# The last stage of a vision and state-space kernel: decays in two pairs of banks, one scan over two groups, the sum added to h by TensorE and ScalarE

## The chip, the cores and the metric

One core of one Trainium2 chip. The metric is the time of one execution on the device in microseconds. All data are float32.

## What is computed

The reference has three parts. A tokenizer (two performer layers between unfoldings of the image) gives tokens h of width 768, 3136 tokens for each of 4 images. Then a selective state-space layer is added to h, and then a routed mixture of 8 experts. Cut to what the change touches:

```
x     = layernorm(h)
Bproj = x @ W_B + b_B;  Cproj = x @ W_C + b_C          # 16 states each
delta = softplus(x @ W_D + b_D + p_Delta)              # one per channel
A_bar = exp(delta * A)
B_bar = (A_bar - A) / (delta * A) * delta * Bproj
state = A_bar * state + B_bar * x                      # over the tokens, in order
y     = sum over the 16 states of Cproj * state
h     = h + y
h     = h + experts(layernorm(h))
```

## The kernel before

Three stages run one after the other. The change is in the third, `tail`. It goes over 28 rounds (`UNITS`, i): 4 images times 7 pieces of 448 tokens (`T`). A round has 24 slots (`STEPS`, k): 6 chunks of 128 channels (dc) times 4 quarters of the states (q). In a slot the 128 partitions hold 32 channels times 4 states, and four groups g of 448 tokens hold the other channels of the chunk. So one slot is 128 x 4 x 448 numbers in one tile of the ring `v` (`RING` = 5 tiles). State by state the work of a slot is:

1. GpSimd, `weigh_in` (L1450): v = x * B, one product of 128 x 1792. It waits until TensorE has read the tile five slots back.
2. ScalarE, `step` (L1691): decay = exp(delta * A) into PSUM, one group at a time, into three banks in turn. The fourth group needs the scan of the first.
3. VectorE, `weigh` (L1793): v = (decay - A) * v, and `scan` (L1802), the recurrence over 448 tokens. Group by group, a scan is issued one `weigh` behind its own, so the last scan of a slot stands behind the first `weigh` of the next and behind all other work of the slot.
4. ScalarE, `keep_states` (L1681): the last column of v goes to `st`, where the scan of the next round starts from. It stands behind the decays of the next slot.
5. GpSimd, `weigh_out` (L1460): v = v * C, again 128 x 1792. GpSimd's order is `weigh_in(k)`, `weigh_out(k-2)`.
6. TensorE, `step` (L1535): four small products sum v over the states into one of two PSUM banks (`YB + dc % 2`), with 1/A as the weights.
7. VectorE, `add_to_h` (L1820): at slots 7, 11, 15, 19, 23 and at slot 3 of the next round, h = h + that bank.

In between, each engine's queue is a list written out by hand: in slot k come the step of round i, then the mixture of experts for the round before (`mlp`, at slots set by `P_...`, `A_...`, `V_...`), then the projection and the delta of the round ahead (`front`). What the steps below speak of:

- TensorE: slot 0 squares of the second layernorm (L1488), slot 1 its mean (L1492), slots 1 to 6 one projection chunk each (L1497, L1499), slot 7 the same for the token means, slots 4 to 8 router and expert products (L1492), slot 11 the product for delta, slots 12 to 15 four masks (L1582), slots 16 to 22 eight output groups of 4 + 1 + 3 products (L1595, L1596, L1598), two of them in slot 18. The first output group waits for the fourth masked expert tile, which VectorE writes in slot 19 (L1870).
- ScalarE: slots 5 to 10 write the projected chunks (L1648), slot 11 the token means (L1651), slot 14 four GELUs between two table loads (L1716, L1717) and the inverse deviation (L1660, L1662), slots 16 to 18 delta (L1668 to L1675), slots 21 to 23 and 0 to 3 of the next round the outputs (L1725). TensorE's squares in slot 0 wait for the last of these, in slot 3.
- VectorE: slots 9 to 12 expert tiles (L1837), 12 routing, 14 the B and C rows (L1775 to L1778), 16 to 19 masks (L1870), 18 and 19 delta (L1784).

```
for g in range(4):
    after(act, s_sc, 4 * n + g - 2)
    fn(bank((4 * n + g) % 3), dr[:, dc % 2, g, :], ACT.Exp,
       scale=aa[:, 4 * k + g:4 * k + g + 1]).then_inc(s_a, 1)
```

## Time and profile before

| | |
|---|---|
| three runs, median | 9341.66 us (9338.44 to 9353.73) |
| profiled execution, its own time | 9346.65 us |
| its span | 9344.9 us |
| TensorE busy | 7616.6 us, 82% |
| VectorE busy | 6306.6 us, 67% |
| ScalarE busy | 4247.4 us, 45% |
| GpSimd busy | 6400.6 us, 68% |
| share of the chain that ended last | TensorE 25%, VectorE 16%, GpSimd 9%, issue 8%, ScalarE 4% |

The span covers all three stages; the third runs from about 3510 us to the end. Shares of the whole span therefore hide it, and the sections below read stretches of the third stage alone. A line number points into the kernel as printed above. In a timeline each row gives the start, the length, engine and line, what is written from what, and in brackets how long the engine stood idle before and who ended that.

### The profile page before, as it was taken

What the parts mean: (1) busy time and instruction counts of PE and PEld (TensorE: products, weight loads), DVE (VectorE), ACT (ScalarE), POOL (GpSimd) and SP (SyncE); (2) the same over time, 40 slices, a digit from 0 to 9 for tenths busy, and PEclk for the clock granted to TensorE, in tenths of its full rate; (3) what the DMA queues carried; (4) which work ended last, traced back from release to release, by engine and by line L of the source; (5) the groups of instructions that cost most, each with busy time, mean ns of one, the idle gap of its engine ahead of it and who ended that gap; (6) DMA issues with size and microseconds to landing.
All of it is one profiled execution on the core that took longest, in us unless ns stands there. A gap on an engine that the chain in (4) does not pass through costs nothing.

```text
span 9344.9 us, 86112 instructions
## 1 busy us (share of the span) xinstructions
PE 7616.6 (82%) x30892; PEld 3189.1 (34%) x30892; DVE 6306.6 (67%) x8010; ACT 4247.4 (45%) x6801; POOL 6400.6 (68%) x2483
## 2 busy tenths in 40 slices
PE   6799999777999985578788778788778788777777
PEld 3444444223444432223333323333323333323333
DVE  1355555441233344888888888888888888888885
ACT  1366666553344432444444444444444444444442
POOL 0011111116766614999999999999999999999995
PEclk9999999998999987788888888888888888888887
DMA  0011111115444413223322323322323322323321
GB/s 25 25 39 43 44 42 38 31 31 105 96 102 97 101 37 99 84 95 115 108 97 91 118 90 119 108 97 89 118 90 118 110 97 89 116 93 112 110 97 51
DMA packets 356851, 786.54 MB, mean 84 GB/s; under 512 B 70437, under 2 KB 282806, under 8 KB 348936
## 3 DMA queue, kind: packets, MB, share of 16 engines
q1 hardware_dynamic: 320376, 690.75, 24.6%
q0 software_dynamic: 21712, 51.75, 2.2%
q10 hardware_dynamic: 14336, 38.54, 1.2%
q8 instruction: 244, 4.00, 0.2%
q14 instruction: 183, 1.50, 0.1%
HBM read 597.36 MB, written 183.35 MB: 84 GB/s over the span
## 4 chain that ended last, share of the span: by engine, by line
PE 25%; DVE 16%; POOL 9%; issue 8%; ACT 4%; DMA 0%; SPq 0%; DVEq 0%; POOLq 0%
PE ps L1492 7%; DVE v L1793 7%; DVE v L1802 7%; PE ps L1499 5%; PE ps L1497 5%; POOL v L1460 5%; POOL v L1450 4%; PE ps L1535 2%; PE ps L1488 2%; PE ps L1595 2%; DVE dl L1784 1%; ACT ps L1691 1%; ACT gm L1716 1%; ACT dl L1668 0%; DVE gm L1870 0%
## 5 line engine op out<-in xcount | busy, mean ns | idle before, releaser
L1691 ACT ACTIVATE ps<-dr,aa 128x448 f32<-128x448 f32 x2688 | 1695.8, 635 | 2649.4 <-DVE v L1802 2631.3
L1450 POOL TENSOR_TENSOR v<-xr,bt 128x1792 f32<-128x1792 f32 x672 | 2683.0, 3993 | 203.2 <-PE ps L1535 105.5
L1460 POOL TENSOR_TENSOR v<-v,ct 128x1792 f32<-128x1792 f32 x672 | 2690.2, 4003 | 177.7 <-ACT st L1681 177.1
L1802 DVE TENSOR_TENSOR_SCAN v<-ps,st,v 128x448 f32<-128x448 f32 x2304 | 2629.1, 1141 | 0.0
L1793 DVE SCALAR_TENSOR_TENSOR v<-ps,aa,v 128x448 f32<-128x448 f32 x2688 | 1786.6, 665 | 660.5 <-POOL v L1450 357.5
L222 POOL DMA_DIRECT2D tokens<-ob x448 | 235.4, 532 | 1883.4 <-ACT ob L383 1833.3
L1595 PE MATMUL ps<-w_or_w,gm 128*112 128x384 f32 x1792 | 737.2, 562 | 453.6 <-DVE gm L1870 382.2
L1535 PE MATMUL ps<-v,dg 128*32 128x448 f32 x5376 | 719.6, 610 | 218.5 <-POOL v L1460 217.9
L1595 PEld LDWEIGHTS ps<-w_or_w,gm 128*112 128x112 f32 x1792 | 340.5, 200 | 867.9 <-DVE gm L1870 424.6
L1492 PE MATMUL ps<-h,w_or_w 128*128 128x448 f32 x1344 | 538.4, 551 | 14.1 <-DVE gm L1837 14.1
L1488 PE MATMUL ps<-sq,jm 128*128 128x448 f32 x672 | 344.7, 658 | 191.2 <-ACT ot L1725 183.3
L1497 PE MATMUL ps<-x,wpa 128*128 128x448 f32 x1008 | 451.7, 584 | 19.7 <-ACT h L1648 14.8
L1499 PE MATMUL ps<-x,wpb 64*128 64x448 f32 x1008 | 449.1, 577 | 0.0
L498 DVE COPY ht<-ps 112x512 f32<-112x512 f32 x112 | 77.5, 692 | 547.5 <-ACT kp L411 547.5
L812 PE MATMUL ps<-xt,wa 128*64 128x448 f32 x2016 | 435.4, 566 | 0.0
L1802 DVE TENSOR_TENSOR_SCAN v<-ps,v 128x448 f32<-128x448 f32 x384 | 415.4, 1082 | 0.0
L1582 PE MATMUL ps<-wpb 9*128 9x448 f32 x224 | 163.1, 822 | 237.3 <-DVE gm L1870 235.0
L1492 PE MATMUL ps<-h,wz 128*128 128x448 f32 x336 | 194.7, 749 | 195.1 <-ACT rs L1660 195.1
L1492 PEld LDWEIGHTS ps<-h,w_or_w 128*128 128x128 f32 x1344 | 248.1, 191 | 305.0 <-issue 287.0
L471 DVE RECIPROCAL qpn<-qpn 128x448 f32<-128x448 f32 x112 | 330.7, 2953 | 3.8
L1535 PEld LDWEIGHTS ps<-v,dg 128*32 128x32 f32 x5376 | 112.3, 113 | 641.1 <-issue 383.3
L1118 DVE TENSOR_TENSOR kq<-ps,rsa 128x896 f32<-128x896 f32 x56 | 61.1, 1092 | 359.6 <-PE ps L820 337.8
(318 smaller groups left out, 11777.1 us busy)
## 6 DMA issues: line engine op xcount, KB each, us to landing
xr<-h_by_channel SPq DMA_DIRECT2D x168, 896.0 KB, 4.7
dr<-delta_by_channel SPq DMA_DIRECT2D x168, 896.0 KB, 5.6
x<-tokens SPq DMA_DIRECT2D x252, 224.0 KB, 5.2
tokens<-ob POOLq DMA_DIRECT2D x448, 112.0 KB, 2.4
w_or_w<-in_w SPq DMA_DIRECT2D x29, 1536.0 KB, 6.3
w_or_w<-centred_w SPq DMA_DIRECT2D x27, 1536.0 KB, 6.4
h_by_channel<-h SPq DMA_DIRECT2D x112, 336.0 KB, 10.8
delta_by_channel<-dl SPq DMA_DIRECT2D x112, 336.0 KB, 5.1
```

Source lines behind the costliest of these rows:

```text
L812: mm(ps[half[g], o, 0:T], wa[:, j, cols], xt[:, 2 * (n % 3) + g, 0:TR2, j:j + 2 * S2 - 1:2], start=(j == 0), stop=False)
L1450: tt(v[:, n % RING], xr[:, dc % 2], bt[:, q:q + 1, :].to_broadcast([128, 4, T]), ALU.mult).then_inc(s_v, 1)
L1460: tt(v[:, n % RING], v[:, n % RING], ct[:, q:q + 1, :].to_broadcast([128, 4, T]), ALU.mult).then_inc(s_cm, 1)
L1488: mm(into, jm[:, :], sq[:, dc % 3, :], start=(dc == 0), stop=(dc == DC - 1)).then_inc(s_var[ln], 1)
L1492: last = mm(into, weights(dc), h[:, i % 3, dc, :], start=(dc == 0), stop=(dc == DC - 1))
L1497: mm(into, even(j), x3[:, 0:TR3, j:j + 2 * S3 - 1:2], start=(j == 0), stop=False)
L1499: last = mm(into, odd(j), x3[0:64, 1:TR3 + 1, j:j + 2 * S3 - 1:2], start=False, stop=(j == 2))
L1535: last = mm(ps[32 * g:32 * g + 32, YB + dc % 2, 0:T], dg[:, 4 * k + g, :], v[:, n % RING, g, :], start=(q == 0), stop=(q == Q - 1))
L1595: mm(into[:, 0:D // 2], gm[:, m, cs], w2[:, m, lo:lo + D // 2], start=(m == 0), stop=False)
L1691: fn(bank((4 * n + g) % 3), dr[:, dc % 2, g, :], ACT.Exp, scale=aa[:, 4 * k + g:4 * k + g + 1]).then_inc(s_a, 1)
L1793: stt(v[:, n % RING, g, :], bank((4 * n + g) % 3), aa[:, 4 * k + g:4 * k + g + 1], v[:, n % RING, g, :], ALU.subtract, ALU.mult).then_inc( ...
L1802: nc.vector.tensor_tensor_scan(v[:, n % RING, g, :], bank((4 * n + g) % 3), v[:, n % RING, g, :], 0.0 if first else st[:, 4 * k + g:4 * k ...
```

## The change

All of it is in `tail`.

- The four decays of a slot go to two pairs of banks, two groups side by side in each pair with one column of zeros ahead of each group (banks 0 to 3; VectorE zeroes all four once). ScalarE writes the first pair when the scan of the first pair of the slot before is done, and the second likewise.
- A tile of v has 449 columns per group. The first column holds the state from which the group starts; ScalarE copies it there from `st` (`start_states`), times 0 at an image's first piece. One scan then runs over two groups, 898 columns, from 0.0. It is issued right behind the two `weigh` of its pair.
- h is added to the sums by a product with the identity on TensorE in the same bank, and ScalarE copies the bank to h (`add_to_h`), ahead of its decays in the same slots as before. There is one bank of sums instead of two, so the first sum of a chunk waits for that copy.
- The ring has 6 tiles. To make room, constants used once lie in `gm`, the third buffer of token means lies in `bcs`, and the squared mean in `rs2`.
- The branches on `OWN` do nothing, since `OWN` is empty: `others(n)` is n + 1.
- The first load of the tail waits until all its buffers are set (`s_set` 6 instead of 1), among them VectorE's zeroing of the banks.

```diff
-RING = 5
-YB, BS, BX, BF = 3, 5, 6, 7
+RING = 6
+AR, YB, BS, BX, BF = 4, 4, 5, 6, 7
+OWN = ()
...
+        def decay(g):
+
+            at = g // 2 * 1024 + g % 2 * (T + 1)
+            return flat[:, at + 1:at + T + 1]
...
-        v = sb("v3", [128, RING, 4, T])
+        v = sb("v3", [128, RING, 4, T + 1])
...
-            sp.wait_ge(s_set, 1)
+            sp.wait_ge(s_set, 6)
...
-                tt(v[:, n % RING], xr[:, dc % 2], bt[:, q:q + 1, :].to_broadcast([128, 4, T]),
+                tt(v[:, n % RING, :, 1:T + 1], xr[:, dc % 2], bt[:, q:q + 1, :].to_broadcast([128, 4, T]),
...
                 if q == 0:
-                    after(pe, s_hy, DC * i + dc - 1)
-                pe.wait_ge(s_cm, n + 1)
+                    after(pe, s_hy, DC * i + dc)
...
                 for g in range(4):
-                    last = mm(ps[32 * g:32 * g + 32, YB + dc % 2, 0:T], dg[:, 4 * k + g, :], v[:, n % RING, g, :],
-                              start=(q == 0), stop=(q == Q - 1))
+                    last = mm(ps[32 * g:32 * g + 32, YB, 0:T], dg[:, 4 * k + g, :], v[:, n % RING, g, 1:T + 1],
+                              start=(q == 0), stop=False)
                 last.then_inc(s_ns, 1)
+                if q == Q - 1:
+                    mm(bank(YB), ident[:, :], h[:, i % 3, dc, :], start=False, stop=True).then_inc(s_hs, 1)
...
+            def start_states(i, k):
+
+                n = STEPS * i + k
+                if k in OWN:
+                    return
+                after(act, s_ns, n + 1 - RING)
+                if i >= 1:
+                    act.wait_ge(s_st, others(n - STEPS))
+                fn(v[:, n % RING, :, 0], st[:, 4 * k:4 * k + 4], ACT.Copy,
+                   scale=0.0 if i % J3 == 0 else 1.0).then_inc(s_s0, 1)
...
+            def add_to_h(i, dc):
+                act.wait_ge(s_hs, DC * i + dc + 1)
+                if dc == 0:
+                    act.wait_ge(s_xst, 64 * (i + 1))
+                fn(h[:, i % 3, dc, :], bank(YB), ACT.Copy).then_inc(s_hy, 1)
...
                 for g in range(4):
-                    after(act, s_sc, 4 * n + g - 2)
-                    fn(bank((4 * n + g) % 3), dr[:, dc % 2, g, :], ACT.Exp,
+                    if g % 2 == 0 and n > 0:
+                        free_pair(n - 1, g // 2)
+                    fn(decay(g), dr[:, dc % 2, g, :], ACT.Exp,
...
+                    if i >= 1 and k == 3:
+                        add_to_h(i - 1, DC - 1)
+                    if i < UNITS and k >= 7 and k % 4 == 3:
+                        add_to_h(i, k // 4 - 1)
                     if i < UNITS:
+                        start_states(i, k)
                         step(i, k)
...
+            def scan(i, k, pair):
+
+                n = STEPS * i + k
+                row = v[:, n % RING, 2 * pair:2 * pair + 2, :].rearrange("p g t -> p (g t)")
+                if pair == 0:
+                    dve.wait_ge(s_s0, others(n))
+                dve.wait_ge(s_wt, 4 * n + 2 * pair + 2)
+                nc.vector.tensor_tensor_scan(row, flat[:, 1024 * pair:1024 * pair + 2 * T + 2], row, 0.0, ALU.mult,
+                                             ALU.add).then_inc(s_sc, 1)
...
+                for pair in range(2):
+                    weigh(i, k, 2 * pair)
+                    weigh(i, k, 2 * pair + 1)
+                    if k in OWN:
+                        own_scan(i, k, pair)
+                    else:
+                        scan(i, k, pair)
...
+            nc.vector.memset(ps[:, 0:AR, :], 0.0).then_inc(s_set, 1)
+            dve.wait_ge(s_set, 6)
```

In these lists of instructions, `L` is the line in the kernel concerned, then comes the operation, and what is written from what. VectorE around slot 19, first before: from the masked tile and delta of slot 18 to those of slot 19.

```order
L1870 TENSOR_TENSOR gm<-gm,ps 128x448
L1784 SCALAR_TENSOR_TENSOR dl<-ps,pd,dl 128x448 x3
L1793 SCALAR_TENSOR_TENSOR v<-ps,aa,v 128x448
L1802 SCALAR_TENSOR_TENSOR v<-ps,st,v 128x448
L1793 SCALAR_TENSOR_TENSOR v<-ps,aa,v 128x448
L1802 SCALAR_TENSOR_TENSOR v<-ps,st,v 128x448
L1793 SCALAR_TENSOR_TENSOR v<-ps,aa,v 128x448
L1802 SCALAR_TENSOR_TENSOR v<-ps,st,v 128x448
L1793 SCALAR_TENSOR_TENSOR v<-ps,aa,v 128x448
L1802 SCALAR_TENSOR_TENSOR v<-ps,st,v 128x448
L1820 TENSOR_TENSOR h<-h,ps 128x448
L1870 TENSOR_TENSOR gm<-gm,ps 128x448
```

And the same place in the changed kernel (L1871 is `weigh`, L1880 the scan, L1861 delta, L1957 the masked tile).

```order
L1957 TENSOR_TENSOR gm<-gm,ps 128x448
L1861 SCALAR_TENSOR_TENSOR dl<-ps,pd,dl 128x448 x3
L1871 SCALAR_TENSOR_TENSOR v<-ps,aa,v 128x448 x2
L1880 SCALAR_TENSOR_TENSOR v<-ps,v 128x898
L1871 SCALAR_TENSOR_TENSOR v<-ps,aa,v 128x448 x2
L1880 SCALAR_TENSOR_TENSOR v<-ps,v 128x898
L1957 TENSOR_TENSOR gm<-gm,ps 128x448
```

Four scans became two, each behind its own pair; the slot's last scan now stands ahead of the slot's other work, and the addition to h is gone from this queue.

ScalarE in slots 22 and 23 before: the decays (L1691), the last states kept (L1681) and the outputs (L1725).

```order
L1691 ACTIVATE ps<-dr,aa 128x448 x4
L1681 ACTIVATE st<-v 128x4
L1725 ACTIVATE ot<-ps 112x384
L1730 DMA out<-ot 112x768
L1691 ACTIVATE ps<-dr,aa 128x448 x4
L1681 ACTIVATE st<-v 128x4
L1725 ACTIVATE ot<-ps 112x384 x2
```

And in the changed kernel (L1733 writes the first states, L1762 the decays, L1723 keeps the last states, L1796 the outputs, L1751 copies the sum to h).

```order
L1733 ACTIVATE v<-st 128x4
L1762 ACTIVATE ps<-dr,aa 128x448 x4
L1723 ACTIVATE st<-v 128x4
L1796 ACTIVATE ot<-ps 112x384
L1801 DMA out<-ot 112x768
L1751 ACTIVATE h<-ps 128x448
L1733 ACTIVATE v<-st 128x4
L1762 ACTIVATE ps<-dr,aa 128x448 x4
L1723 ACTIVATE st<-v 128x4
L1796 ACTIVATE ot<-ps 112x384 x2
```

The copy to h stands ahead of slot 23's decays, and each slot has one small write more.

## Rows read from the trace of the kernel before

**Rows 1.** Two stretches: busy PE, PEld, DVE, ACT, POOL; TensorE's granted clock; DMA.
```profile
5000.00:6000.00 1000.00, 789.99 (x2740) 315.62 (x2740) 865.66 (x1136) 455.24 (x843) 948.08 (x240) 0.86 0.31 104
...
7178.00:7210.00 32.00, 9.07 (x30) 1.58 (x28) 30.12 (x40) 18.24 (x30) 31.07 (x9) 0.52 0.02 8
```

**Rows 2.** Timeline of GpSimd: start, length, what, [idle before, who ended it].
```profile
3637.50 11.80 POOL L1450 TENSOR_TENSOR v<-xr,bt 128x1792 f32<-128x1792 f32 x3 [97.70 <-DMA xr<-h_by_channel]
...
7035.94 3.99 POOL L1450 TENSOR_TENSOR v<-xr,bt 128x1792 f32<-128x1792 f32 x1 [0.97 <-PE ps L1535]
...
7132.33 3.99 POOL L1450 TENSOR_TENSOR v<-xr,bt 128x1792 f32<-128x1792 f32 x1 [1.17 <-PE ps L1535]
...
7142.85 3.99 POOL L1450 TENSOR_TENSOR v<-xr,bt 128x1792 f32<-128x1792 f32 x1 [1.99 <-PE ps L1535]
...
7174.79 4.00 POOL L1460 TENSOR_TENSOR v<-v,ct 128x1792 f32<-128x1792 f32 x1 [3.25 <-ACT st L1681]
...
9239.80 3.97 POOL L1460 TENSOR_TENSOR v<-v,ct 128x1792 f32<-128x1792 f32 x1 [0.30 <-ACT st L1681]
```

**Rows 3.** Timeline of TensorE; x counts each float32 product twice.
```profile
7009.36 5.46 PE L1595 MATMUL ps<-w_or_w,gm 128*112 128x384 f32 x8 [14.39 <-DVE gm L1870]
...
7017.57 2.83 PE L1595 MATMUL ps<-w_or_w,gm 128*112 128x384 f32 x8
...
7028.66 4.53 PE L1595 MATMUL ps<-w_or_w,gm 128*112 128x384 f32 x8 [1.28 <-ACT ot L1725]
...
7034.78 0.96 PE L1535 MATMUL ps<-v,dg 128*32 128x448 f32 x8
...
7068.22 4.85 PE L1488 MATMUL ps<-sq,jm 128*128 128x448 f32 x6 [7.48 <-ACT ot L1725]
...
7074.03 4.78 PE L1492 MATMUL ps<-h,jm 128*128 128x448 f32 x12
...
7098.18 0.96 PE L1535 MATMUL ps<-v,dg 128*32 128x448 f32 x8
```

**Rows 4.** Timeline of ScalarE.
```profile
7141.89 0.62 ACT L1651 ACTIVATE mu<-ps,mub 9x448 f32<-9x448 f32 x1 [5.07 <-PE ps L1499]
7142.54 1.19 ACT L1691 ACTIVATE ps<-dr,aa 128x448 f32<-128x448 f32 x2
...
7162.24 1.28 ACT L1716 ACT_TABLE_LOAD   x1
...
7167.86 0.58 ACT L1662 ACTIVATE rs<-rs 128x448 f32<-128x448 f32 x1
```

**Rows 5.** Timeline of VectorE.
```profile
7143.28 0.69 DVE L1793 SCALAR_TENSOR_TENSOR v<-ps,aa,v 128x448 f32<-128x448 f32 x1 [3.03 <-ACT ps L1691]
7143.88 1.14 DVE L1802 TENSOR_TENSOR_SCAN v<-ps,st,v 128x448 f32<-128x448 f32 x1
...
7149.84 0.60 DVE L1837 TENSOR_TENSOR gm<-ps,rs2t 128x448 f32<-128x448 f32 x1
...
7150.77 0.17 DVE L1854 RECIPROCAL sm<-sm 112x4 f32<-112x4 f32 x1
...
7168.47 0.62 DVE L1775 TENSOR_TENSOR ps<-ps,rs 48x448 f32<-48x448 f32 x1 [3.13 <-ACT rs L1662]
7169.13 0.67 DVE L1777 SCALAR_TENSOR_TENSOR bcs<-ps,bbc,rs 16x448 f32<-16x448 f32 x1
...
7194.23 0.68 DVE L1793 SCALAR_TENSOR_TENSOR v<-ps,aa,v 128x448 f32<-128x448 f32 x1 [1.88 <-ACT ps L1691]
...
7210.14 0.61 DVE L1870 TENSOR_TENSOR gm<-gm,ps 128x448 f32<-128x448 f32 x1
```

**Rows 6.** Page, costliest groups (busy us, mean ns): scans with and without a pointer start.
```profile
L1802 DVE TENSOR_TENSOR_SCAN v<-ps,st,v 128x448 f32<-128x448 f32 x2304 | 2629.1, 1141 | 0.0
...
L1802 DVE TENSOR_TENSOR_SCAN v<-ps,v 128x448 f32<-128x448 f32 x384 | 415.4, 1082 | 0.0
```

**Rows 7.** Timeline of GpSimd, before the last stage's first product.
```profile
3534.45 5.36 POOL L1469 TENSOR_TENSOR dg<-sel,ai 128x3072 f32<-128x3072 f32 x1 [15.95 <-DVE pd L1875]
```

More of the change, by code:

```diff
@@ L1158, with others, owned @@
 UNITS = B * J3
-RING = 5
-YB, BS, BX, BF = 3, 5, 6, 7
+RING = 6
+AR, YB, BS, BX, BF = 4, 4, 5, 6, 7
+OWN = ()
 FEW = NX + 1
 CAP = 30.0
+def others(n):
+    i, k = divmod(n, STEPS)
+    return i * (STEPS - len(OWN)) + sum(j not in OWN for j in range(k + 1))
+def owned(n):
+    return n + 1 - others(n)
 def tail(nc, sem, w, c, t2, w1c, xd, dd, bcd, out):
@@ L1174, in bank, with decays @@
             return ps[rows, k, 0:n]
+        flat = ps[:, :, :].rearrange("p k n -> p (k n)")
+        def decay(g):
+            at = g // 2 * 1024 + g % 2 * (T + 1)
+            return flat[:, at + 1:at + T + 1]
+        def decays(pair):
+            row = flat[:, 1024 * pair:1024 * pair + 2 * T + 2]
+            return row.rearrange("p (g t) -> p g t", g=2)[:, :, 1:T + 1]
         ident = sb("ident3", [128, 128])
         jm = sb("jm768", [128, 128])
-        sel32 = sb("sel32", [128, 32])
         desc = sb("desc", [CH, NCH, NX])
@@ L1314, in tail, with means @@
         ROUTE, TAIL = 9, 28
+        def means(i):
+            return mu[few, i % 3, :] if i % 3 < 2 else bcs[few, :]
         def pair_bank(o):
@@ L1384, in spread_c @@
                 if i < UNITS:
-                    after(sp, s_cm, STEPS * (i - 1) + STEPS - Q + q + 1)
+                    for own in (True, False):
+                        k = max((k for k in range(q, STEPS, Q) if (k in OWN) == own), default=None)
+                        if i >= 1 and k is not None:
+                            n = STEPS * (i - 1) + k
+                            sp.wait_ge(s_cv if own else s_cm, 2 * owned(n) if own else others(n))
                     spread_row(ct[:, q, :], i, 1, q).then_inc(s_lc[q], 16)
@@ L1702, in mlp @@
                     act.wait_ge(s_mean, i + 1)
[L1703 removed]
+                    fn(rs2[:, :], bank(BX), ACT.Square).then_inc(s_ms, 1)
                 if k == A_RS2:
@@ L1791, in weigh @@
                     dve.wait_ge(s_v, n + 1)
-                dve.wait_ge(s_a, 4 * n + g + 1)
-                stt(v[:, n % RING, g, :], bank((4 * n + g) % 3), aa[:, 4 * k + g:4 * k + g + 1], v[:, n % RING, g, :],
-                    ALU.subtract, ALU.mult).then_inc(s_wt, 1)
-            def scan(i, k, g):
+                dve.wait_ge(s_a, 4 * n + g // 2 * 2 + 2)
+                row = v[:, n % RING, g, 1:T + 1]
+                stt(row, decay(g), aa[:, 4 * k + g:4 * k + g + 1], row, ALU.subtract, ALU.mult).then_inc(s_wt, 1)
@@ L1797, in scan @@
                 n = STEPS * i + k
                 first = i % J3 == 0
-                if g == 0 and not first:
-                    dve.wait_ge(s_st, n + 1 - STEPS)
-                dve.wait_ge(s_wt, 4 * n + g + 1)
-                nc.vector.tensor_tensor_scan(v[:, n % RING, g, :], bank((4 * n + g) % 3), v[:, n % RING, g, :],
-                                             0.0 if first else st[:, 4 * k + g:4 * k + g + 1], ALU.mult,
-                                             ALU.add).then_inc(s_sc, 1)
@@ L1806, in step @@
-            def step(i, k):
-                for g in range(4):
-                    weigh(i, k, g)
-                    if g > 0:
-                        scan(i, k, g - 1)
-                    elif k > 0:
-                        scan(i, k - 1, 3)
-                    elif i > 0:
-                        scan(i - 1, STEPS - 1, 3)
-            def add_to_h(i, dc):
-                dve.wait_ge(s_ns, STEPS * i + Q * (dc + 1))
-                if dc == 0:
-                    dve.wait_ge(s_xst, 64 * (i + 1))
-                tt(h[:, i % 3, dc, :], h[:, i % 3, dc, :], bank(YB + dc % 2), ALU.add).then_inc(s_hy, 1)
+                if not first:
+                    dve.wait_ge(s_sv, 2 * owned(n - STEPS) + pair - 1)
@@ new lines, in own_scan @@
+                for g in range(2 * pair, 2 * pair + 2):
+                    dve.wait_ge(s_wt, 4 * n + g + 1)
+                    nc.vector.tensor_tensor_scan(decay(g), decay(g), v[:, n % RING, g, 1:T + 1],
+                                                 0.0 if first else st[:, 4 * k + g:4 * k + g + 1], ALU.mult,
+                                                 ALU.add).then_inc(s_sp, 1)
+                if k // Q == 0 and pair == 0:
+                    dve.wait_ge(s_lc[k % Q], 16 * (i + 1))
@@ new lines, in own_scan @@
+                dve.wait_ge(s_sp, 4 * owned(n) + 2 * pair - 2)
+                tt(v[:, n % RING, 2 * pair:2 * pair + 2, 1:T + 1], decays(pair),
+                   ct[:, k % Q:k % Q + 1, :].to_broadcast([128, 2, T]), ALU.mult).then_inc(s_cv, 1)
+            def step(i, k):
+                for pair in range(2):
+                    weigh(i, k, 2 * pair)
+                    weigh(i, k, 2 * pair + 1)
+                    if k in OWN:
+                        own_scan(i, k, pair)
+                    else:
+                        scan(i, k, pair)
@@ L1909, in _ @@
                         step(i, k)
-                    elif k == 0:
-                        scan(UNITS - 1, STEPS - 1, 3)
-                    if i >= 1 and k == 3:
-                        add_to_h(i - 1, DC - 1)
-                    if i < UNITS and k >= 7 and k % 4 == 3:
-                        add_to_h(i, k // 4 - 1)
                     if i >= 2 and k + STEPS < TAIL:
```

48 lines of the change are left out of this document (33 added, 15 removed).

## The prediction

> **What bounds the kernel now.** I read busy times first. In a steady stretch of the last stage, 5000 to 6000 us, GpSimd is busy 95% of the time, VectorE 87%, TensorE 79%, ScalarE 46% [rows 1]. That looks like a kernel bound by GpSimd with little left to win. VectorE's masked tile of slot 19 ends at 7210.75 [rows 5], and TensorE had started on the one of the round before at 7009.36 [rows 3]: a round takes 201.4 us. In GpSimd's timeline, from 7035.94 to 7132.33 GpSimd does 24 products with one stall of 1.17 [rows 2], so a product takes a place of (96.39 - 1.17) / 24 = 3.97 us, and 48 of them 190.6 us. A round therefore holds 10.8 us of stalls. The stage runs from 3637.50 to 9243.77, 5606 us; 28 x 190.6 = 5337; the excess of 269 is 25 full rounds of stalls. The first two rounds and the last lack part of the other work. More than 269 us can't be won unless GpSimd's own products change.
>
> The stalls of GpSimd are symptoms, ended by TensorE or ScalarE. The timelines of the other engines show a loop through three stretches that adds up to the round:
> - A to S, 58.9 us: from TensorE's first output group (7009.36, idle 14.39 until VectorE's last masked tile) to its squares at 7068.22, idle 7.48 until ScalarE's last output copy of slot 3 [rows 3].
> - S to W, 75.1 us: TensorE works nearly without a gap until the token means, which ScalarE, idle 5.07, takes at 7141.89; it writes decays, and VectorE starts slot 12 at 7143.28 after an idle of 3.03 [rows 3 to 5].
> - W to A, 67.5 us: VectorE alone, slots 12 to 19, with waits of 3.13 and 1.88 for ScalarE, up to the masked tile whose end (7210.75) starts the next output group [rows 5].
>
> 58.9 + 75.1 + 67.5 = 201.5, the round. GpSimd is only nearly the bound.
>
> **A slot on VectorE.** Four `weigh` and four scans take 7149.84 - 7143.28 = 6.56 us [rows 5]. A `weigh` takes a place of 0.58 to 0.60, since its 0.665 overlaps the next instruction, and a scan the rest, 1.05, of a length of 1.141. Without a pointer start a scan is 1.082 [rows 6]. No scan of 898 columns is in the trace. Bounds: one scan of 448, 1.08, and two, 2.16. The smallest vector instruction takes 0.17 [rows 5], so I take 0.15 as the fixed part that two scans share once: 2.16 - 0.15 = 2.02, near the upper end. The scan now needs the `weigh` just ahead of it. Such a pair stands at 7168.47 (0.62) and 7169.13 [rows 5]: 0.04 after the end, with no overlap, so the second `weigh` costs 0.70. A pair of groups is 0.58 + 0.70 + (2.02 - 0.08) = 3.22, a slot 6.45. **The merged scan gains only 0.1 us a slot.** At the upper bound each scan costs 0.14 more; 24 scans lie in the 12 slots that count below, so a round would be 3.4 us longer than the forecast's.
> The Trainium skill (VectorE: DVE Perf Modes, "The DRAIN you can't avoid") says that a semaphore between vector instructions costs nothing, as the pipe is flushed in any case. Here the rows disagree by 0.12 us; by the rule the round would be another 24 x 0.12 = 2.9 us shorter.
>
> **W to A.** VectorE loses two additions to h (slots 15 and 19), each 0.5 by its spacing from the next, like the tiles of 0.6 in [rows 5]: -1.0. The wait of 1.88 at slot 18 goes, since ScalarE's delta work now runs while VectorE is in the same slot: its decays no longer wait for the slot's own first scan, so its other work starts about 4 us sooner. The wait of 3.13 in slot 14 ends with the inverse deviation at 7168.44, 6.2 us after ScalarE starts on its table load at 7162.24 [rows 4]; it now starts 1.5 us into the slot (two decays and the kept states), so it ends at 7.7, and VectorE arrives at 6.45 + 0.65 = 7.1: 0.6 is left, -2.5. Eight slots at -0.1: -0.8. Sum 67.5 - 6.2 = **61.3**.
>
> **S to W.** Two identity products (slots 3 and 7). Six products of 128 x 448 take 4.78 [rows 3], one 0.8: +1.6. VectorE now waits for two decays, which take 1.19 [rows 4], instead of one: +0.6. The copies to h and the first states (0.6 and 0.1) lie in ScalarE's waits for TensorE. **77.3**.
>
> **A to S.** Here the change adds a wait. ScalarE copies chunk 4 to h ahead of slot 23's decays, and that needs the sums of slot 19, which TensorE does after four output groups: 7034.78 + 0.96 is 26.4 after A [rows 3]. Their wait of 1.28 for ScalarE goes: 25.1; identity +0.8; copy, first states, two decays and the hand-overs 2.0: VectorE starts slot 23 at 27.9. It would be ready at 1.8 (delta) + 3 x 6.45 = 21.2. So **VectorE waits 6.7 us for ScalarE in slot 23**, and what is queued behind that copy (slot 23's decays, the kept states of slot 22, an output) waits too; GpSimd stalls about 1 us for those states. Then four slots, 25.8, and ScalarE's two decays, kept states and output, 2.0: S at **55.7**. TensorE's last output group and slot 23's sums and identity end before that, at about 48.
>
> Sum: 55.7 + 77.3 + 61.3 = 194.3, against 201.4: 7.1 less, above GpSimd's 190.6. The sixth tile removes GpSimd's waits for TensorE (0.97, 1.17, 1.99, [rows 2]), which were part of the same loop and give nothing more. Times 25: -178 us.
>
> **The rest.** GpSimd's products now write rows with gaps. Nothing of that form is in the trace; the nearest, with both inputs in rows of 32, takes 5.36 us for 3072 [rows 7], less per element than 3.99 for 1792, so I take 0, with up to +0.1 a product as the other end: GpSimd's round is then 195.4. Zeroing the four banks is 2048 columns on VectorE's path ahead of the first projection: between 0.2 and 4 us, I take +2. The earlier load wait is covered by the constants. The small writes are 0.1 to 0.2 each on ScalarE, idle half the time, and stand in its waits: 0; without that cover 24 x 0.1 a round.
>
> -176 on the profiled execution's 9346.65 gives 9171; that execution lies 5 above the median, and against 9341.66 it is **9166 us**.
>
> **Rivals.**
> - *Forecast*, the loop shortens to between 191.9 (one clock effect of the next case) and 197.7: 0.61. The upper end (scans at 2.16) gives 9341.66 - 3.7 x 25 + 2 = 9251.
> - *GpSimd becomes the bound.* For it: TensorE's granted clock is 0.52 from 7178 to 7210 us [rows 1], its lower level of 1.2 GHz for most of a stretch in which it was busy 9.07 of 32 us, and that lasts past A. At S too, after an idle of 7.48, six rows of squares took 4.85, where twelve rows of the mean took 4.78 just after, and the output group at 7028.66 took 4.53 against 2.83 [rows 3]. Shorter idles may bring both back, 2.4 + 1.7. The loop is then 190.2 and GpSimd's 190.6 decides: 9342 - 10.8 x 25 + 2 = 9074. Chance 0.20.
> - *One bank of sums takes the gain away.* TensorE can't start a chunk's sums before ScalarE's copy, in its queue at the slot where that queue already waits. It comes to slot 4's sums at 7098.18 [rows 3], one projection of 5.2 us behind slot 3's; the copy takes 0.7 of that, if ScalarE is there. From 4.5 us of lateness each further one lengthens the round, and 11.6 undo everything: about 9340. Against it: before slots 12, 16 and 0 TensorE waits for something else anyway. Chance 0.08. The Trainium skill (Perfetto Trace Analysis, "Matmuls") says that groups of products should rotate through banks so that emptying one overlaps the next group; by it this change is a step back, and the time would be this rival's.
> - *Slower: TensorE at its lower clock behind A.* The new wait in slot 23 hangs on TensorE's speed from A to slot 19, which before had slack. From the first output group to the second it is 7017.57 - 7009.36 = 8.2 [rows 3]; with the halves that are at full speed, 5.3. If the next three stay slow, +2.9, +2.9 and +2 with the sums and identity, and two groups of six at S as well (+4.6), the round is 194.3 + 12.4 = 206.7: 9342 + 5.3 x 25 + 2 = 9476. It decides from 7.1 us. For it: the idle of 14.39 before A stays. Against: at 7017.57 a row of the same eight takes 2.83 again. The chance is 0.11, in which I also count a scan over two banks that costs over 2.32 us.
>
> **Numbers.** A measurement of this kernel tells 0.2%, 19 us, from no change. Faster 0.61 + 0.20 = 0.81, same 0.08, slower 0.11. Range 9060 to 9290: the GpSimd bound with some us below, the forecast's upper end, and a partly lengthened loop.
>
> **What would show it.** GpSimd's same stall 194 us apart; scans of 898 columns at 2.0 us; no wait for TensorE on GpSimd; a wait of VectorE for ScalarE's decays of 5 to 8 us in slot 23, and under 1 us in slots 14 and 18; TensorE's sums of slots 4, 8 and 12 not waiting for the copy. The forecast is wrong if scans cost over 2.2, if GpSimd's products leave 3.97, or if the wait in slot 23 is absent or over 10.

## The result and the profile after

The changed kernel takes **9094.36 us** (median of four runs, 9085.56 to 9098.78) against 9346.51 for the kernel before in the same comparison: ratio 0.9729, 95% interval 0.9712 to 0.9746. Forecast were 9166 us and a range of 9060 to 9290. The sign and the likeliest mechanism held, and the gain is 252 us where 176 were expected: one term of the round was too large by 2 us, and what the forecast put at nothing (the sixth tile, GpSimd's products, the first and the last round) gave something.

Busy times in the steady stretch 5000 to 6000, to be held against [rows 1] (columns as there):
```profile
5000.00:6000.00 1000.00, 847.37 (x2928) 337.32 (x2929) 877.27 (x907) 487.65 (x1040) 953.24 (x252) 0.90 0.32 108
```
GpSimd is as busy as before (953 against 948) although its work per round shrank: a round got shorter too. The costliest groups of the page:
```profile
L1880 DVE TENSOR_TENSOR_SCAN v<-ps,v 128x898 f32<-128x898 f32 x1344 | 2725.5, 2028 | 92.4
L1482 POOL TENSOR_TENSOR v<-xr,bt 128x1792 f32<-128x1792 f32 x672 | 2690.0, 4003 | 98.4 <-DMA xr<-h_by_channel 98.4
L1494 POOL TENSOR_TENSOR v<-v,ct 128x1792 f32<-128x1792 f32 x672 | 2475.4, 3684 | 239.6 <-ACT st L1723 238.9
```
The scan of 898 columns takes 2.03 us, as forecast. The second product of GpSimd takes 3.68, where it took 4.00 [rows 2]; the forecast had no change or a longer one.

**The three stretches of a round.** TensorE's timeline from A (first output group, 7054.98) to S (squares, 7108.44) and the next A:
```profile
7054.98 5.21 PE L1635 MATMUL ps<-w_or_w,gm 128*112 128x384 f32 x8 [10.23 <-DVE gm L1957]
...
7062.67 2.83 PE L1635 MATMUL ps<-w_or_w,gm 128*112 128x384 f32 x8
...
7067.99 2.83 PE L1635 MATMUL ps<-w_or_w,gm 128*112 128x384 f32 x8
...
7072.32 2.74 PE L1635 MATMUL ps<-w_or_w,gm 128*112 128x384 f32 x8
...
7076.66 0.96 PE L1573 MATMUL ps<-v,dg 128*32 128x448 f32 x8
7081.99 2.83 PE L1635 MATMUL ps<-w_or_w,gm 128*112 128x384 f32 x8 [3.43 <-ACT ot L1796]
...
7104.91 0.96 PE L1573 MATMUL ps<-v,dg 128*32 128x448 f32 x8 [0.63 <-ACT h L1751]
7108.44 4.85 PE L1523 MATMUL ps<-sq,jm 128*128 128x448 f32 x6 [2.57 <-ACT ot L1796]
...
7247.61 4.47 PE L1635 MATMUL ps<-w_or_w,gm 128*112 128x384 f32 x8 [10.23 <-DVE gm L1957]
```
ScalarE's timeline in slot 23, and VectorE's at the start of slot 23, at the start of slot 12 (W) and in slot 14:
```profile
7078.60 0.54 ACT L1751 ACTIVATE h<-ps 128x448 f32<-128x448 f32 x1 [7.09 <-PE ps L1577]
7079.04 0.20 ACT L1733 ACTIVATE v<-st 128x4 f32<-128x4 f32 x1
7079.14 2.30 ACT L1762 ACTIVATE ps<-dr,aa 128x448 f32<-128x448 f32 x4
```
```profile
7080.43 1.28 DVE L1871 SCALAR_TENSOR_TENSOR v<-ps,aa,v 128x448 f32<-128x448 f32 x2 [4.12 <-ACT ps L1762]
...
7186.06 1.28 DVE L1871 SCALAR_TENSOR_TENSOR v<-ps,aa,v 128x448 f32<-128x448 f32 x2 [2.57 <-ACT ps L1762]
...
7208.32 0.62 DVE L1852 TENSOR_TENSOR ps<-ps,rs 48x448 f32<-48x448 f32 x1 [0.43 <-ACT rs L1702]
```
This gives, for the round from 7054.98:

| stretch | before | forecast | after |
|---|---|---|---|
| A to S | 58.9 | 55.7 | 53.5 |
| S to W | 75.1 | 77.3 | 77.6 |
| W to A | 67.5 | 61.3 | 61.5 |
| round | 201.4 | 194.3 | 192.6 |

The round quoted is a long one of the changed kernel: its full rounds last between 190.5 and 193.9 us.

**Slots, a second measure.** From VectorE's timeline I took the end of the last scan of every slot; the distance from the one before it is the slot's time, with all waits and all other work in it. Means over rounds 5 to 24 (us), and the mean round over the 25 full rounds:
```
kernel                      0     1     2     3     10     14     15     22     23    round
before                    7.89  7.88  7.89  7.86  10.28  12.48   7.56   7.09   8.73  200.97
changed                   6.53  6.53  6.53  7.54  11.97   6.53   9.79   6.53  10.55  191.86
```
The last scan of a slot stood behind the slot's other work and the first `weigh` of the next slot; now it stands ahead of that work. So other work, and a wait at the start of a slot, count one slot earlier in the row before. Slots 14 and 15 have to be read together (20.04 and 16.32), and so have 22 and 23 (15.82 and 17.08): the wait that the change brings at the start of slot 23 is in them.

Twenty-five full rounds at -9.1 are -228 us; the first round (185.9 to 175.1) gives -11, what lies behind the full rounds -19, and the first slot ends 7 us later. Sum -251 up to the last scan, in the two profiles. The end of the first slot lies between 3637.8 and 3656.5 in the profiles of this study, also between kernels that are the same up to there, so between two experiments less than 20 us apart I compare the rounds, not the totals.

### The profile page after: what moved, and what is told of

Same layout as the page of the kernel before. It is cut to its first block, busy times and chain, and to the rows that moved or that the text cites. A ratio compares the mean times of both kernels' runs of the same rounds, so it can differ in the third digit from the quotient of the medians.

```text
span 9093.5 us, 86859 instructions
## 1 busy us (share of the span) xinstructions
PE 7714.0 (85%) x31228; PEld 3228.1 (35%) x31228; DVE 6128.7 (67%) x6499; ACT 4307.8 (47%) x7641; POOL 6188.6 (68%) x2484
## 4 chain that ended last, share of the span: by engine, by line
PE 33%; DVE 14%; ACT 5%; issue 5%; POOL 3%; DMA 0%; SPq 0%; DVEq 0%; ACTq 0%; POOLq 0%
PE ps L1527 7%; PE ps L1635 6%; DVE v L1880 6%; DVE v L1871 5%; PE ps L1534 5%; PE ps L1532 5%; PE ps L1573 3%; ACT ps L1762 3%; PE ps L1523 2%; POOL v L1482 2%; PE ps L1638 2%; PE ps L1636 2%; POOL v L1494 1%; PE ps L1577 1%; DVE dl L1861 1%
## 5 line engine op out<-in xcount | busy, mean ns | idle before, releaser
L1880 DVE TENSOR_TENSOR_SCAN v<-ps,v 128x898 f32<-128x898 f32 x1344 | 2725.5, 2028 | 92.4
L1494 POOL TENSOR_TENSOR v<-v,ct 128x1792 f32<-128x1792 f32 x672 | 2475.4, 3684 | 239.6 <-ACT st L1723 238.9
L1762 ACT ACTIVATE ps<-dr,aa 128x448 f32<-128x448 f32 x2688 | 1586.0, 627 | 1554.8 <-DVE v L1880 1537.7
L1871 DVE SCALAR_TENSOR_TENSOR v<-ps,aa,v 128x448 f32<-128x448 f32 x2688 | 1691.2, 671 | 560.5 <-ACT ps L1762 501.0
L1688 ACT ACTIVATE h<-ps,pbias 128x448 f32<-128x448 f32 x168 | 106.4, 633 | 711.5 <-PE ps L1534 711.5
L1523 PE MATMUL ps<-sq,jm 128*128 128x448 f32 x672 | 315.6, 611 | 63.3 <-ACT ot L1796 56.8
L276 PE MATMUL ps<-wki,h 128*112 128x256 f32 x896 | 287.0, 404 | 21.3 <-DVE hu L493 21.3
```

The costliest lines, as they stand in the source:

```text
L1494: tt(v[:, n % RING, :, 1:T + 1], v[:, n % RING, :, 1:T + 1], ct[:, q:q + 1, :].to_broadcast([128, 4, T]), ALU.mult).then_inc(s_cm, 1)
L1523: mm(into, jm[:, :], sq[:, dc % 3, :], start=(dc == 0), stop=(dc == DC - 1)).then_inc(s_var[ln], 1)
L1762: fn(decay(g), dr[:, dc % 2, g, :], ACT.Exp, scale=aa[:, 4 * k + g:4 * k + g + 1]).then_inc(s_a, 1)
L1871: stt(row, decay(g), aa[:, 4 * k + g:4 * k + g + 1], row, ALU.subtract, ALU.mult).then_inc(s_wt, 1)
L1880: nc.vector.tensor_tensor_scan(row, flat[:, 1024 * pair:1024 * pair + 2 * T + 2], row, 0.0, ALU.mult, ALU.add).then_inc(s_sc, 1)
```

## The experiments

All but the first and `f3_h_alone` start from the changed kernel. Lines with + and - are the whole edit or its core. An experiment that stands on another one names it.

**1. The gap alone** (`e1_gap_alone`), on the kernel before.
```diff
-        v = sb("v3", [128, RING, 4, T])
+        v = sb("v3", [128, RING, 4, T + 1])
-                tt(v[:, n % RING], v[:, n % RING], ct[...
+                tt(v[:, n % RING, :, 1:T + 1], v[:, n % RING, :, 1:T + 1], ct[...
```
(and `1:T + 1` at every other use of v).


> The kernel before with one part of the change alone: the rows of v are 449 apart, nothing else. Asked: is the gap the cause of the second product's 3.68 us (4.00 before), and is that time worth anything by itself. Loop theory: the product takes 3.68 here too, the round stays 201.4 us as GpSimd only stalls longer, and only the two first rounds and the last, which GpSimd sets, are 24 x 0.32 = 7.7 shorter: about -21, 9325 us. Rival, GpSimd's products count in every round: 28 x 7.7 = -215, 9130 us. If the product takes 4.00, the gap is not the cause and the time is that of before.

Measured: 9293.85 us, ratio 0.994 (0.9924 to 0.9956). GpSimd's groups:
```profile
L1450 POOL TENSOR_TENSOR v<-xr,bt 128x1792 f32<-128x1792 f32 x672 | 2686.8, 3998 | 252.5 <-PE ps L1535 157.2 <-DMA xr<-h_by_channel 95.0
L1460 POOL TENSOR_TENSOR v<-v,ct 128x1792 f32<-128x1792 f32 x672 | 2475.9, 3684 | 280.4 <-ACT st L1681 280.3
```
The gap brings the 3.68. In this kernel it is worth 54 us: a full round falls from 200.97 to 199.20, the first one by 7.3. That is between the theories, nearer to the loop: of the 7.7 us that GpSimd saves in a round 1.8 arrive. Slots 0 to 3, in which VectorE waits for GpSimd's first product, go from 7.9 to 7.6 us each.

**2. Is it contiguity** (`e4_full_rows`), **or where the input begins** (`g3_x_one_column_off`, on the kernel of experiment 8)**?**
```diff
+        ct = sb("ct", [128, Q, T + 1])
+                tt(v[:, n % RING], v[:, n % RING], ct[:, q:q + 1, :].to_broadcast([128, 4, T + 1]),
```
```diff
-        xr = sb("xr", [128, 2, 4, T])
+        xr = sb("xr", [128, 8 * T + 1])[:, 1:8 * T + 1].rearrange("p (a g t) -> p a g t", a=2, g=4)
```


> The changed kernel, but GpSimd's second product runs over whole rows of 449 with the gap column (contiguous, 1796 elements, the extra column multiplied and never read). Asked: what the faster product is worth. Loop theory: the product is back at 4.0 us, GpSimd's round at 24 x 7.94 = 190.6 against the loop's 191.9, so full rounds lengthen by 0 to 1 and three rounds by 7.7: +21 to +48, 9115 to 9142. Rival, GpSimd sets the round of the changed kernel: 28 x 7.7 = +215, 9309. If the product stays at 3.7, contiguity is not what matters.

> The kernel of 8937 us with the tile of h by channel (first input of GpSimd's first product) starting one column later, its rows still 448 apart. Asked: what makes the second product 3.68 us where it was 4.00. If it is where its first input begins, the first product is now 3.68 too, GpSimd's round 24 x 7.36 = 177 instead of 184.4 of 185.6, and the round falls by up to 3 us (the loop is next): 8860 to 8920. If it is that output and input are the same tile, or its rows' gap, the first product stays 4.00 and the time 8937.

Measured: 9084.78 us (0.9725 of before, 0.9709 to 0.9741; a round 191.7) and 8924.37 us (0.9542, 0.9528 to 0.9557).
```profile
L1494 POOL TENSOR_TENSOR v<-v,ct 128x1796 f32<-128x1796 f32 x672 | 2485.0, 3698 | 229.1 <-ACT st L1724 228.7
```
```profile
L1482 POOL TENSOR_TENSOR v<-xr,bt 128x1792 f32<-128x1792 f32 x672 | 2687.8, 4000 | 94.3 <-DMA xr<-h_by_channel 94.3
```
Over contiguous rows of 449 the product stays fast (first fence), and the other product stays at 4.00 with its first input one column off and its output in gapped rows (second fence). So it is not that the rows have gaps, and for the first product an input that starts one column later is not enough. What is common to the fast cases is that rows 449 apart are read as well as written; whether it is that, or reading and writing the same tile in such rows, stays open. No run gave the first product an input in rows of 449. Since the first experiment here did not bring back 4.00 us, it does not tell what the faster product is worth in the changed kernel. The second's 12 us against 8936.74 lie in the start (3639.9 against 3656.1), its full rounds are the same (185.65 against 185.72).

**3. The sixth tile** (`f1_five_tiles`): `RING = 5`.


> The changed kernel with five v tiles instead of six. The prediction said that GpSimd's waits for TensorE's sums are part of the same loop, so the sixth tile gives nothing: within 20 us of 9094. Rival: the sixth tile lets GpSimd run ahead of VectorE over the stretch in which TensorE is late with its sums. In the kernel before VectorE's slots 0 to 3 took 7.9 us each and in the changed one 6.5, and slots 0 to 3 lie on the stretch A to S: with five tiles they are back at GpSimd's pace of 7.6, +4 x 1.1 = 4.4 a round, +110, 9204.

Measured: 9124.91 us (0.976, 0.9745 to 0.9774), 31 more than with six. GpSimd's longest wait and VectorE's wait for GpSimd from 5000 to 9000 (sum in us, times, longest), with five tiles:
```profile
POOL v L1482 <- PE ps L1573: 207.7, 113, 4.8
...
DVE v L1871 <- POOL v L1482: 131.6, 164, 1.1
```
with six:
```profile
POOL v L1494 <- ACT st L1723: 185.8, 102, 4.3
DVE v L1871 <- POOL v L1482: 19.8, 29, 1.0
```
and VectorE's in the kernel before:
```profile
DVE v L1793 <- POOL v L1450: 235.6, 220, 2.0
```
With five tiles GpSimd waits for TensorE's sums again, VectorE waits for GpSimd 6 us a round instead of 1, and its slots 1, 2 and 4 take 6.78, 7.27 and 7.57 instead of 6.53 each: the rival's mechanism, but only 1.0 us of it reaches the round, not 4.4.

**4. The merged scan** (`f2_split_scans`).
```diff
-                nc.vector.tensor_tensor_scan(row, flat[:, 1024 * pair:1024 * pair + 2 * T + 2], row, 0.0, ...
+                nc.vector.tensor_tensor_scan(row[:, 0:half], flat[:, at:at + half], row[:, 0:half], 0.0, ...
+                nc.vector.tensor_tensor_scan(row[:, half:2 * half], flat[:, at + half:at + 2 * half], ...
```


> The changed kernel with each scan of 898 columns split into two of 449 (same banks, same order, same waits). Theory: a merged scan takes 2.03, two single ones have places of 1.05 and 2 x 1.05 = 2.10 against 2.03 - 0.08, so +0.15 a pair, +0.3 a slot; some 14 slots of a round are at VectorE's own pace: +4.2 a round, +105, 9199. Rival, the merged scan gives nothing and the gain of the change is its order and banks: within 20 us of 9094.

Measured: 9110.16 us (0.9741, 0.9726 to 0.9755), 16 more; a round 192.22 against 191.86.
```profile
L1881 DVE TENSOR_TENSOR_SCAN v<-ps,v 128x449 f32<-128x449 f32 x1344 | 1469.0, 1093 | 92.3
L1883 DVE TENSOR_TENSOR_SCAN v<-ps,v 128x449 f32<-128x449 f32 x1344 | 1433.3, 1066 | 0.0
```
Two scans have 2.16 us against 2.03, but a slot at VectorE's own pace grows only from 6.53 to 6.63, since the second scan starts 0.08 us before the first ends. The rival holds ("within 20"), and the theory's 0.3 us a slot was wrong. **The merged scan is worth under 0.2%.**

**5. h alone** (`f3_h_alone`), on the kernel before: identity product in TensorE, copy by ScalarE ahead of the slot, two banks of sums kept.
```diff
+                if q == Q - 1:
+                    mm(bank(YB + dc % 2), ident[:, :], h[:, i % 3, dc, :], start=False, stop=True).then_inc(s_hs, 1)
+                fn(h[:, i % 3, dc, :], bank(YB + dc % 2), ACT.Copy).then_inc(s_hy, 1)
-                tt(h[:, i % 3, dc, :], h[:, i % 3, dc, :], bank(YB + dc % 2), ALU.add).then_inc(s_hy, 1)
```


> The kernel before with one part of the change alone: h is added in TensorE by the identity product and copied back by ScalarE ahead of the slot's decays (two banks of sums kept). Theory: VectorE loses four additions on its stretches (-2.0) and gains the wait in slot 23 for the decays queued behind the copy, some 6 us of which 2 are there before (slot 23 takes 8.7): +2 a round, +50, 9398. Rival: VectorE's work is what counts, -3 a round, -75, 9272.

Measured: **9517.85 us, ratio 1.0182 (1.0166 to 1.0197): slower by 169.** VectorE's timeline in slot 23:
```profile
7129.61 0.69 DVE L1806 SCALAR_TENSOR_TENSOR v<-ps,aa,v 128x448 f32<-128x448 f32 x1 [7.20 <-ACT ps L1700]
```
The wait ahead of slot 23's first `weigh` is 6.7 us in the mean, where it was 0.5 and for GpSimd. By the last scans, slots 22 and 23 together take 19.8 us instead of 15.8, and slot 0 9.5 instead of 7.9. The theory was right in sign and too small by a factor of three: it counted the 8.7 us of slot 23 as a wait for ScalarE that was there before, but that time lies ahead of slot 0's first `weigh`, which waits for GpSimd (1.6 us in the mean). What queues behind ScalarE's late copy reaches slot 0 too.

**6. The copy of slot 23 behind its decays** (`e2_copy23_behind`).
```diff
-                    if i < UNITS and k >= 7 and k % 4 == 3:
+                    if i < UNITS and k >= 7 and k % 4 == 3 and k != 23:
                         add_to_h(i, k // 4 - 1)
...
                     elif i < UNITS and k > 0:
                         keep_states(i, k - 1)
+                    if i < UNITS and k == 23:
+                        add_to_h(i, k // 4 - 1)
```


> The changed kernel, ScalarE's copy to h of slot 23 placed behind that slot's decays and the kept states instead of ahead of them. Theory (A to S is set by VectorE, which waits 4.1 us in slot 23 for the decays queued behind that copy): the wait goes, S comes 4.1 earlier, the round is 187.8 instead of 191.9, -100 us, 8993. Rival, TensorE sets A to S and the wait lies in its shadow: within 20 us of 9094. Rival, the later copy holds TensorE's sums of slot 20 and so GpSimd's ring: slower than 9094.

Measured: 8976.59 us (0.9606, 0.9592 to 0.9621). Slot 23 takes 6.53 instead of 10.55; the full rounds are 187.85 instead of 191.86, -100 together, and 15 more lie in the start. The wait was on the path at its full 4 us. GpSimd's stalls shrink with it, from 185.8 to (5000 to 9000):
```profile
POOL v L1494 <- ACT st L1723: 106.1, 80, 2.4
```

**7. The copies by VectorE, late and early** (`e3_copy_by_vector`, `g1_vector_copies_early`). In both VectorE copies and ScalarE doesn't. The first does it where the additions stood, at the slot's end; the second ahead of the slot, in slot 23 behind it:
```diff
+                    if i >= 1 and k == 3:
+                        add_to_h(i - 1, DC - 1)
+                    if i < UNITS and k >= 7 and k % 4 == 3 and k != 23:
+                        add_to_h(i, k // 4 - 1)
                     if i < UNITS:
                         step(i, k)
+                    if i < UNITS and k == 23:
+                        add_to_h(i, k // 4 - 1)
```


> The changed kernel with the six copies to h of a round given back to VectorE, where the additions stood before; the sum stays in TensorE. Theory (loop): the slot-23 wait of 4.1 us goes, four copies of 0.5 us (slots 15, 19, 23, 3) lie on VectorE's stretches: -4.1 + 2.0 = -2.1 a round, -52 us, 9042. Rival, VectorE's busy time is what counts and the wait is shadowed: 6 x 0.5 x 25 = +75, 9169.

> VectorE copies the sums to h, but at the place where ScalarE does it in the kernel of 8977 us: ahead of the slot's own work in slots 3, 7, 11, 15 and 19, behind it in slot 23. The copies by VectorE at the ends of these slots gave 9343. Theory, one bank of sums makes the place of the copy decide, and not the engine: only four copies of 0.5 us come onto VectorE's stretches, 187.7 + 2 a round, about 9030. Rival, the engine decides (VectorE reaches these places about a slot later than ScalarE and then stands in the wait itself): the round stays over 197, above 9230.

Measured: **9342.69 us late** (0.9995 of before, 0.9986 to 1.0005), **8985.84 us early** (0.9611, 0.9596 to 0.9625). TensorE's timeline of the late one:
```profile
7060.69 1.72 PE L1573 MATMUL ps<-v,dg 128*32 128x448 f32 x8 [8.79 <-DVE h L1903]
7095.11 1.72 PE L1573 MATMUL ps<-v,dg 128*32 128x448 f32 x8 [2.33 <-DVE h L1903]
...
7176.14 1.72 PE L1573 MATMUL ps<-v,dg 128*32 128x448 f32 x8 [3.69 <-DVE h L1903]
7206.68 1.72 PE L1573 MATMUL ps<-v,dg 128*32 128x448 f32 x8 [14.89 <-DVE h L1903]
```
and TensorE's waits for the copy from 5000 to 9000, late, early, and in the changed kernel:
```profile
PE ps L1573 <- DVE h L1903: 593.9, 99, 14.9
```
```profile
PE ps L1573 <- DVE h L1903: 244.7, 81, 12.1
```
```profile
PE ps L1573 <- ACT h L1751: 71.0, 41, 10.8
```
My expectation for the late one was wrong by 300 us: it counted the copies' own time and not what TensorE's sums of the next chunk wait for, though slot 23's wait did go (6.53 there). With one bank of sums and the copies at the slot's end TensorE waits for them 30 us a round, a round takes 201.39 us, and the whole gain of the change is gone. With five of the six moved ahead of their slot, the same engine gives 187.92 a round, against 187.85 with ScalarE; TensorE still waits 12 us a round for them, and that does not reach the round. **The place decides, not the engine.** That it is the single bank which makes the late place costly is read from TensorE's waits alone, since no run has the late copies in the new order with two banks: in the kernel before, with two, TensorE waited 2.3 us in the whole run for the additions at these places.

**8. The scan one instruction later** (`f4_scan_one_later`), on the kernel of experiment 6.
```diff
+                weigh(i, k, 0)
+                weigh(i, k, 1)
+                weigh(i, k, 2)
+                scan(i, k, 0)
+                weigh(i, k, 3)
+                scan(i, k, 1)
```


> The changed kernel with ScalarE's slot-23 copy behind the decays (8977 us) and the first scan of a slot one instruction later, behind the third weigh, so that it needs nothing from the instruction just ahead. Theory: a dependent pair costs 0.12 us more, one of the two in a slot goes: slots of 6.53 become 6.41, 14 of them in a round, -1.7, -42 us, 8935. Rival: the first pair's decays come 0.6 later for ScalarE, which is then the one that VectorE waits for: +0.5 a slot, slower than 8977. Rival, GpSimd (24 x 7.68 = 184.4 of 187.7) takes the gain: within 15 of 8977.

Measured: **8936.74 us, ratio 0.9557 (0.954 to 0.9574)**, 0.4% under experiment 6 and with it 4.4% under the kernel before. A round is 185.72, and GpSimd is busy 98% of it. Slots with other work of VectorE's between them fell by 0.2 (16 to 18 from 7.06 to 6.86, 19 and 20 from 8.83 to 8.64), bare ones stay at 6.52. VectorE's timeline of a bare slot and of one behind a tile:
```profile
6969.77 2.03 DVE L1873 SCALAR_TENSOR_TENSOR v<-ps,aa,v 128x448 f32<-128x448 f32 x3
...
6939.63 1.86 DVE L1873 SCALAR_TENSOR_TENSOR v<-ps,aa,v 128x448 f32<-128x448 f32 x3
```
In the bare slot the third `weigh`, now 2 us earlier, meets its decays 0.17 late, and that eats the gain. That the total is as expected (8937, 8935) is luck: the full rounds gave -53 us and not -42, from other slots and at 0.2 instead of 0.12 each, and this profile's first slot ended 16 us later than that of experiment 6. The rival on ScalarE's decays holds in the bare slots, without a loss. That it is 0.2 and not 0.12 shows in the changed kernel's slot 16, where the first scan starts 0.11 us behind the end of its second `weigh` and the second scan 0.03; with the overlap of 0.08 that such a pair lacks, the one that went cost 0.19:
```profile
7217.46 1.27 DVE L1871 SCALAR_TENSOR_TENSOR v<-ps,aa,v 128x448 f32<-128x448 f32 x2
7218.84 2.03 DVE L1880 TENSOR_TENSOR_SCAN v<-ps,v 128x898 f32<-128x898 f32 x1
7220.78 1.25 DVE L1871 SCALAR_TENSOR_TENSOR v<-ps,aa,v 128x448 f32<-128x448 f32 x2
7222.06 2.03 DVE L1880 TENSOR_TENSOR_SCAN v<-ps,v 128x898 f32<-128x898 f32 x1
```
Both this kernel and that of experiment 6 beat both kernels of the study.

**9. TensorE's idle filled** (`g2_filled_idle`, `h1_filled_to_a`).
```diff
+            def fill(count):
+                for _ in range(count):
+                    mm(ps[0:32, YB, 0:128], zeros[:, :], jm[:, :], start=False, stop=False)
...
+                        if m == 2 and i + 1 < UNITS:
+                            fill(10)
...
                     if o == 0:
+                        if i + 1 < UNITS:
+                            fill(18)
```
(32 in the second).


> The changed kernel, with TensorE kept busy in its two last idles before the first output group: 10 products of zeros (128 columns, added to the open sums) ahead of the third mask, 18 ahead of the first output group. Asked: is the clock behind that idle part of A to S. Theory: the first two output groups take 2.8 instead of 5.4, slot 19's sums come some 5 us sooner, the slot-23 wait of 4.1 goes, -4 a round, -100, 8994. Rival: the granted clock at A stays at its lower level: 9094, or later if the products of zeros last beyond A.

> As the kernel with TensorE's idles filled, but with 32 products of zeros ahead of the first output group instead of 18, so that they end some 2 us before it and not 5.0. With 18 the granted clock was full over the products and back at 0.50 when the first output group began, which took 5.46 as without them. Theory: the clock now stays full over the shorter idle, the first output group takes 2.8, slot 19's sums and with them slot 23's decays come 2.4 us sooner, and all of it goes into the round: -2.4 x 25 = -60, 9034. Rival, TensorE's time from A to slot 19's sums isn't what sets the round: 9094 even with a first group of 2.8.

Measured: 9081.51 us (0.9711, 0.9694 to 0.9727) and 9075.65 us (0.971, 0.9693 to 0.9726). TensorE's busy time and granted clock in stretches of 2 us with 18 products, up to A at 7042.27:
```profile
7034.00:7036.00 2.00, 2.00 (x17) 0.83 0.00 0
7036.00:7038.00 2.00, 1.31 (x13) 1.00 0.00 0
7038.00:7040.00 2.00, 0.00 (x0) 1.00 0.00 0
7040.00:7042.00 2.00, 0.00 (x0) 0.88 0.00 0
7042.00:7044.00 2.00, 1.73 (x3) 0.50 0.00 0
```
The granted clock rises from 0.50 (1.2 GHz) to 1.00 (2.4 GHz) during these products, but within the idle of 4.96 behind them it falls again, and the first output group takes 5.46. With 32, TensorE's timeline reads:
```profile
7017.66 7.97 PE L1583 MATMUL ps<-jm,zeros 128*32 128x128 f32 x64
7028.12 2.83 PE L1645 MATMUL ps<-w_or_w,gm 128*112 128x384 f32 x8 [2.48 <-DVE gm L1967]
...
7038.75 2.83 PE L1645 MATMUL ps<-w_or_w,gm 128*112 128x384 f32 x8
...
7044.70 2.83 PE L1645 MATMUL ps<-w_or_w,gm 128*112 128x384 f32 x8 [1.45 <-ACT ot L1806]
```
The clock stays full and the group takes 2.83, but the round falls by 0.6 us only (191.30), and the wait in slot 23 from 3.9 to 3.5 in the mean: the fourth output group now waits 1.45 for ScalarE's output copy, which stands in a slot and so at VectorE's pace. The theory's first half held, its second did not. In the totals, 13 and 19 us under 9094, the different starts (6 and 18 us earlier in the profiles) are most of it.

## Why the prediction was right, and where not

- **The loop, not GpSimd, sets the round.** Held. The one wait that the forecast put on the path, in slot 23, gave back all of its 4 us when it was taken away (experiment 6), and GpSimd's saving of 7.7 us a round gave 1.8 (experiment 1). But the loop is not free of GpSimd: in the kernel before VectorE's slots 0 to 8 take 7.9 to 8.0 us, GpSimd's pace, with a wait for it of 0.7 to 1.6 us in each, and slots 0 to 2 and part of slot 3 lie between A and S. The prediction called GpSimd's stalls symptoms; its slots of 6.45 there were right for the kernel after, without saying that they had been 7.9.
- **W to A**, 61.3: 61.5. The wait of slot 14 is 0.43 (0.6 forecast), that of slot 18 gone, the additions gone. That the sum is so close is partly luck: the eight slots gave 0.2 instead of 0.8, and the two waits and the two additions 0.4 more than counted. **S to W**, 77.3: 77.6.
- **A to S**, 55.7: 53.5. This term was mis-sized. The new wait in slot 23 is there, through the chain that was named (sums of slot 19, identity, ScalarE's copy, decays), but it is 4.1 us and not 6.7. The forecast took TensorE's way from A to the end of the identity product from the row before, 25.9 us, with a fourth output group at 4.53 [rows 3]. It is 7078.60 - 7054.98 = 23.6: the fourth group took 2.74, and from the first group to the second it is 7.7 us instead of 8.2. Granted clock around the fourth group, before and after:
```profile
7028.00:7030.00 2.00, 1.34 (x3) 0.74 0.69 184
7030.00:7032.00 2.00, 2.00 (x5) 0.50 0.31 103
```
```profile
7072.00:7074.00 2.00, 2.00 (x11) 1.00 1.00 353
```
The forecast removed the wait of 1.28 us ahead of that group and kept the duration at the lower clock that had come behind it. Why the clock fell there stays open: the changed kernel keeps it over the idle of 3.43 ahead of the fifth group (2.83 again), while in the two kernels of experiment 9 the same group takes 5.46 behind the same 3.43. The rest of the 2.6 us: from the copy to VectorE's start it is 1.83 instead of 2.0, and VectorE was ready 0.1 later. In the kernel of experiment 5, which keeps the old order, the wait is 7.2.
- **The slower rival** (TensorE at its lower clock behind A) did not come about: behind the first group the next three took 2.83, 2.83 and 2.74. The rival with GpSimd as the bound named two gains of the clock, 1.7 for the fourth output group and 2.4 at S. The first came, the second didn't (4.85 again for the squares). So the mean round of 191.9 lands on the forecast's lower end by the other of the two effects than the one priced there, and that is partly luck.
- **Slot on VectorE**, 6.45: 6.53, and the scan 2.02: 2.03. The gain of 0.1 us a slot did not come: slots with nothing else in them, 20 and 21, took 6.50 before. The merged scan does give its 0.10 (experiment 4), and the scan right behind the `weigh` it depends on takes it back. The Trainium skill (VectorE: DVE Perf Modes, "The DRAIN you can't avoid") says that a semaphore between vector instructions costs nothing. Experiment 8 goes against that for a neighbour that needs the result: one such pair fewer took 0.2 us from each slot in which the decays were there in time.
- **One bank of sums takes the gain away.** Rejected with 0.08, and for the placing chosen in the change that is right: TensorE waits 3.4 us a round for the copy. Experiment 7 shows how near it was: with the copies behind their slot's work the gain is gone. The prediction counted the projection of 5.2 us as margin; the late copies bring waits of up to 14.9. The Trainium skill (Perfetto Trace Analysis, "Matmuls") advises that groups rotate through banks, so that emptying one overlaps the next group. With one bank TensorE did wait, 30 us a round in the late placing and 12 in the early one; only the first reached the round.
- **The sixth tile gives nothing.** Wrong by 31 us (experiment 3): GpSimd's waits for TensorE were passed on to VectorE in slots that lie on the loop.
- **GpSimd's products with gapped rows, 0 to +0.1.** Wrong: -0.32 for one of the two. The nearest row, with both inputs in rows of 32, said nothing about it. Alone it is worth 54 us; what it is worth in the changed kernel was not isolated, since no edit tried brought the old duration back.
- **Outside the full rounds** nothing but +2 was counted. The first round gave -11 and the last ones -19. The +2 for zeroing the banks had no row; the first slot ended 7 us later than before, which is within what that point varies by.

So the missing 76 us are 2.0 us a round (50), of which the mis-sized wait is more than the whole, and some 25 outside the full rounds, where GpSimd sets the pace. What the new order and the bank pairs give by themselves was not tried: four banks of decays leave one for sums, and with that one bank and the copy at its old place (experiment 7) nothing of the gain is left. From the parts that were tried (+169 for h alone and -54 for the gap, on the kernel before; 16 and 31 lost when the scan or the tile is taken back from the changed one) it is clear only that the gain is not a sum of parts.

## What to carry to other kernels

Where an in-order queue takes over work, price what stands behind it in that queue at every place where it is issued: one of six equal copies cost 4 us a round, and moving it behind the slot's own work gave 1.1%; what the other five cost in ScalarE's queue was not measured. A single buffer between two engines can cost nothing where it is emptied early and the whole gain where it is emptied at the end of the step, so try the place before the engine. And a duration read at the lower clock is a bound and not a price: when the schedule around it changes, give the sum with that duration and with the one at full clock, for the runs here show both behind an idle of the same length.
